# Fifty small warm-up products in place of twenty-two large ones at the head of a fused linear-attention and FFN kernel

## The reference

```python
x = x + attn(layernorm(x), Wq, bq, Wk, bk, Wv, bv, Wo, bo)
# attn, 16 heads of 16 features:
q = elu(x @ Wq.T + bq) + 1;  k = elu(x @ Wk.T + bk) + 1;  v = x @ Wv.T + bv
# for each chunk of tokens:
scores = where(tril, q @ k.T, 0)
num = scores @ v + q @ S;  den = sum(q * (cumsum(k) + z))
S, z = S + k.T @ v, z + k.sum
out = (num / den) @ Wo.T + bo
x = x + ffn(layernorm(x), ...)
# ffn, weights dequantized from integers with scales per group of 128:
x + 0.5 * (silu(h @ w1 + b1) @ w2 + b2),  h = norm(x) * gamma + beta
```

## Time and profile before

| | us |
|---|---|
| median of 3 runs | 1653.42 |
| the three runs | 1665.78, 1652.40, 1653.42 |
| the profiled execution, its own time | 1655.49 |
| its span, first to last instruction | 1653.8 |
| PE busy | 1469.5 (89%), 25690 matmuls, as many weight loads |
| DVE busy | 1225.5 (74%) |
| ACT busy | 1069.1 (65%) |
| POOL busy | 686.6 (42%) |
| mean granted TensorE clock | 0.968 of 2.4 GHz |

### The profile page before, as it was taken

How to read it: one execution, slowest core, us unless ns; L and a number is a source line. 1 busy time by engine, 2 the same in 40 slices (tenths; PEclk the granted TensorE clock), 3 DMA queues, 4 the chain that set the end, 5 groups by cost and what they waited for, 6 DMA issues and landing times. The chain is left out here.

```text
span 1653.8 us, 60762 instructions
## 1 busy us (share of the span) xinstructions
PE 1469.5 (89%) x25690; PEld 1270.1 (77%) x25690; DVE 1225.5 (74%) x2014; ACT 1069.1 (65%) x1789; POOL 686.6 (42%) x473
## 2 busy tenths in 40 slices
PE   7599898989889998989998989899899898889988
PEld 7577788777778777878777788777788777777867
DVE  5587677867777876777877768867778866778855
ACT  4475567766667756667766667756677765676753
POOL 2143245433445433445443345433445433355443
PEclk8799899999999999999999999999999999999999
DMA  5112111122121122121122121122121122111110
GB/s 142 37 36 54 39 42 40 42 54 54 29 53 37 45 54 54 28 54 36 45 54 54 29 53 32 50 54 54 29 53 33 49 54 53 29 42 39 41 41 26
DMA packets 93790, 76.22 MB, mean 46 GB/s; under 512 B 8768, under 2 KB 92992, under 8 KB 93504
## 3 DMA queue, kind: packets, MB, share of 16 engines
q1 hardware_dynamic: 92144, 71.59, 17.1%
q10 hardware_dynamic: 1360, 0.01, 0.0%
HBM read 38.03 MB, written 16.78 MB: 33 GB/s over the span
## 5 line engine op out<-in xcount | busy, mean ns | idle before, releaser
L985 POOL TENSOR_TENSOR s_lo<-silu_f,s_hi 128x512 fp32r<-128x512 f32 x256 | 347.6, 1372 | 679.3 <-ACT s_hi L844 679.3
L837 ACT ACTIVATE silu_f<-silu_f 128x512 f32<-128x512 f32 x256 | 156.9, 625 | 73.5 <-DVE silu_f L626 73.5
L636 DVE TENSOR_TENSOR probs<-sc,causal 128x1024 f32<-128x1024 f32 x128 | 150.6, 1218 | 56.6 <-PE sc L416 56.6
L292 PE MATMUL num<-w_hi,s_hi 128*128 128x256 f32 x496 | 148.3, 299 | 41.8 <-DVE phi_q L597 41.8
L844 ACT ACTIVATE s_hi<-silu_f 128x512 fp32r<-128x512 f32 x256 | 152.2, 620 | 0.1
L292 PE MATMUL num<-w_lo,s_hi 128*128 128x256 f32 x496 | 145.1, 293 | 0.0
L292 PE MATMUL num<-w_hi,s_lo 128*128 128x256 f32 x496 | 145.1, 292 | 0.0
L292 PE MATMUL sc<-w_hi,s_hi 128*128 128x256 f32 x496 | 143.4, 289 | 0.0
L292 PE MATMUL sc<-w_lo,s_hi 128*128 128x256 f32 x496 | 140.2, 283 | 0.0
L292 PE MATMUL sc<-w_hi,s_lo 128*128 128x256 f32 x496 | 140.1, 282 | 0.0
L292 PEld LDWEIGHTS num<-w_hi,s_hi 128*128 128x128 f32 x496 | 100.0, 202 | 47.7 <-DVE phi_q L597 47.7
(11 more groups left out here) (193 smaller groups left out, 4648.9 us busy)
## 6 DMA issues: line engine op xcount, KB each, us to landing
x_in<-in_x SPq DMA_DIRECT2D x32, 512.0 KB, 3.6
rb<-den_rows SPq DMA_DIRECT2D x256, 64.0 KB
xb<-in_x SPq DMA_DIRECT2D x32, 512.0 KB, 4.9
out<-out_t SPq DMA_DIRECT2D x64, 256.0 KB, 4.2
probs<-in_q SPq DMA_DIRECT2D x2, 512.0 KB, 8.1
silu_f<-in_q SPq DMA_DIRECT2D x2, 512.0 KB, 6.3
res<-in_sc SPq DMA_DIRECT2D x1, 512.0 KB, 6.9
out_t<-in_sc SPq DMA_DIRECT2D x1, 512.0 KB, 11.0
```

The lines of the kernel that those rows point to most:

```text
L292: last = e.matmul(target, a, b, start=(n == 0), stop=(n == 3 * len(pairs) - 1))
L636: masked.done(e.tensor_tensor(probs[:, t, 2 * h:2 * h + 2, :, :, :].rearrange("p g m a q -> p (g m a) q"), sc[:, 2 * h:2 * h + 2, :].rearr ...
L837: silu.done(e.activation(slot, slot, ACT.Silu))
L985: sl.done(e.tensor_tensor(s_lo[:, j, :], silu_f[:, j % SLOTS, :], s_hi[:, j, :].bitcast(F32), ALU.subtract))
```

## The change

`WARM` becomes 50, and each of these products takes 64 columns of the identity as weights and 64 as the moving operand, where it took 128 and 128; the contraction stays 128 long. The result is 64x64 in the same bank. `keep_busy` keeps its size, and nothing else changes.

```diff
-    WARM, WARM_BETWEEN = 22, 5
+    WARM, WARM_BETWEEN = 50, 5
...
             def first_transposes():
                 for n in range(WARM):
-                    e.matmul(bank(SPARE)[:, 0:P], ident[:, :], ident[:, :], start=True, stop=True)
+                    e.matmul(bank(SPARE)[0:HALF, 0:HALF], ident[:, 0:HALF], ident[:, 0:HALF], start=True, stop=True)
                 for c in range(C):
```

## The result

| | before | after |
|---|---|---|
| median of four runs each, us | 1652.91 | 1544.56 |
| lowest and highest, us | 1641.20, 1665.78 | 1540.54, 1550.07 |
| profiled execution: its own time, span, us | 1655.49, 1653.8 | 1540.54, 1538.8 |
| mean granted TensorE clock | 0.968 | 0.986 |

A forecast was written before the change was run, and what follows sets the result against it. PE, with stops for 256-instruction code pieces, was taken to bound the kernel. Lead-in 0 and 0, loop +6, batch 0 -1.5, last batch -2 sum to +2.5 us: 1658.0 profiled, 1656 as median, range 1640 to 1672.

The forecast's parts named there:

- What bounds the kernel: Whole kernel: PE, busy 89% of the span, decides most of a batch and outruns delivery of its 256-instruction code pieces.
- Part 1: Lead-in: 100 small matmuls replace 44; at half price, 34 fit the low-clock time and the last ends near 9.9 us.
- Parts 2 and 3: Lead-in: delay to the transposes and ScalarE's copy, and gain from a higher clock there; both taken as 0.
- Part 4: Loop: piece edges fall 56 pairs earlier; new stops 2.4 us against 2.2, +0.2 a batch, +6 us over 29 passes.
- the prediction's own sign of being wrong: Loop: wrong if batches keep their old stops or the mean batch changes by over 0.6 us.
- Part 5: Batch 0 and last batch: stops move with the edges, -1.5 us and -2 us.
- The rivals: Whole kernel: slower 1686 (0.12), faster 1631 (0.10), nothing moves 1653 (0.12), warm-up cases up to 1658 or 1662 (0.06).
- the faster one: Loop: code deliveries come early wherever PE was not stopped before, as at the head (2.7 us); 1631 us, chance 0.10.
- the step's own test: Whole run: instruction packets fall from 278 to about 250, one a pass fewer.
- Its other sign: Loop batch: no stop in first scores or state products; one over 1 us at fc1 behind the first values.

The follow-up runs named there:

- E9: The kernel after with 27 tiny 32x32 products put ahead of one fc1 group in each loop pass; 1555.89 us.
- E2: The kernel before with 50 warm-up products of the old, large size in place of 22; 1542.42 us.
- E6: The kernel before with 14 large warm-up products in place of 22; 1561.43 us.
- E11: The kernel before with 17 large warm-up products in place of 22; 1639.75 us.
- E7: The kernel before with 37 large warm-up products in place of 22; 1792.63 us.

## Why the prediction was wrong

It said 1656 and no change, and gave "faster by over 1%" 0.11. Step by step:

- **What bounds the kernel**: right. PE, pieces of 256 instructions, stops called "issue", 16 KB each. The stop at the head of a pass was in its rows too.
- **Part 1, the small products**: the price was right, the time at the low clock was not. 9.9 us was the predicted end, 11.3 is measured. By the starts of the products, 54 of the 100 matmuls ran at the low clock, 0.107 us apart, and the rest at 0.058 (54 x 0.107 + 46 x 0.058 = 8.4 of 8.61), not 34. The clock rose 5.7 us after the first product; in the kernel before it rose after 3.3 us and 15 large ones, not 17. It isn't the size that does it: the same 100 small products end at 10.15 us in E9, with a rise after 3.2 us, and in E2 the large ones wait 5.2 us for theirs. So an end of 9.9 was near one of these traces and 1.4 off in the other, with no effect on the time in either.
- **Parts 2 and 3**: right, both 0. ScalarE still began at 15.05. The transposes found the clock high in the trace after and low in that of E9, and ScalarE began at 14.88 there.
- **Part 4, the loop**: this step failed. It moved the edges to the right places and priced what each delivery would cost at the new ones: stops of 1.55, 0.8 and 0.1 us. Under that lies the assumption that "every edge then falls 56 pairs earlier" and that all else stays: that each pass fetches its code anew, because it did so before. It was never asked why a loop fetched the same code 29 times, with 278 packets in plain sight, nor what it would take for it not to. The runs show that a pass whose code fits has no deliveries at all. So the 2.2 us of old stops were not replaced by 2.4 of new ones, they went; and the 1.48 us at the head, which the part used only as an old value to be kept, went with them. The part's sum was +0.2 a batch with -0.65 as its best bound; measured it is -3.9, new waits included. Its 2.2 us of old stops were also read from one pass and left out the head; the prediction's own sign of being wrong, a mean batch that changes by over 0.6 us, is met.
- **Part 5, outside the loop**: the edges landed where it put them. In call 0:

```profile
39.76 0.79 PE L446 MATMUL num<-probs,v_pad 64*32 64x64 f32 x57
43.04 2.11 PE L446 MATMUL num<-probs,v_pad 64*32 64x64 f32 x127 [2.49 <-issue]
46.47 1.32 PE L446 MATMUL num<-probs,v_pad 64*32 64x64 f32 x72 [1.32 <-issue]
47.73 1.72 PE L460 MATMUL num<-phi_q,state 32*32 32x64 f32 x56
50.31 1.09 PE L460 MATMUL num<-phi_q,state 32*32 32x64 f32 x56 [0.86 <-issue]
51.33 0.66 PE L331 MATMUL sc<-ident,x_hat 128*128 128x128 f32 x4
```

Breaks after 57 of the first values, 56 of the second (127 - 71), 56 of the states, as forecast. The state products end near 51.4 instead of the forecast 50.6, 0.9 us earlier than before where 1.5 was forecast. But in the trace of E9, with the same code up to there, they end at 54.3, later than before, so neither figure is borne out. In the last batch it hoped for 2 us by having the edges beside fc1; there the stops are still there, the largest of them in the values and in the states:

```profile
1475.83 1.01 PE L446 MATMUL num<-probs,v_pad 64*32 64x64 f32 x78 [0.89 <-issue]
...
1483.61 1.44 PE L460 MATMUL num<-phi_q,state 32*32 32x64 f32 x75 [0.92 <-issue]
```

As a picture of where the edges fall in code that runs once, the step was sound, and its sizes were a microsecond or so. It was applied to code that runs 29 times.
- **The rivals**: the faster one, 1631, had the right sign for another reason (early deliveries) and a fifth of the size. None was "the loop stays in place". The count of packets was the step's own test, "about 250, one a pass fewer"; it came out at 26. Its other sign came true for a reason that it didn't have: no stop splits the state products, because none is left; and the stop behind the first values that it looked for isn't there.
- The rule in "Runtime: NRT & Kernel Launch" of the Trainium skill that crossing a block is "mostly hidden" isn't borne out here: with 9 packets a pass this loop loses 3.9 us of 50.

## What to carry to other kernels

If a loop's instruction packets are about its passes times its pieces, its code doesn't stay on the engine, and the question is how many instructions it is over, not where the stops fall: in these runs a body on PE stayed when it touched at most 7 pieces of 256, which depends on its length and on where it begins. Before tuning anything inside such a loop, add or delete a few instructions ahead of it and look at the packet count; here one product more or less moved the time between 1537, 1561 and 1793 us. And compare variants that change the number of instructions ahead of a loop only with that count beside the time, since otherwise an edit in the first microseconds is credited with what the alignment did.

## What the runs showed of the hardware

- PE held 8 pieces, 2048 instructions: 25 to 27 packets a run in all eight kernels whose body touched 7, 278 or 279 in the five whose body went clearly into an eighth.
- One piece too many costs the whole loop: nine packets and 4.1 us each time (E6). Throwing out the oldest piece or the one used longest ago would both do this; the runs don't tell them apart.
- The piece ahead is asked for shortly after one is entered: with the branch 2 instructions in, in 6 passes (E6); 14 in, in all (E11).
- A stop of 5 us for code is followed by a stretch at clock 0.50 (E7, 5.6 us in the window shown), so a badly placed head pays twice.
- The same 100 warm-up matmuls took 8.61 us in one trace and 7.48 in another (after, E9, the same code up to the loop), as the clock rose 5.7 or 3.2 us after the first. When it rises is not fixed by the program alone.
